# Last stage: GpSimd adds the first three of a token's six rows, VectorE the other three

## What is computed

```
for each expert e:  routed += combine[:, e] * (silu(g) * u @ down[e].T)      # six experts per token
sh = silu(xf @ shared_gate_w.T) * (xf @ shared_up_w.T)
shared_out = sh @ shared_down_w.T
x = x + gb * (routed + shared_out)                                           # gb: one row per batch
```

## Time and profile before

| | |
|---|---|
| time, median of 3 runs | 1427.1 us (1426.59 to 1427.19) |
| the profiled execution | 1430.49 us, its span in the trace 1428.7 us |
| busy over the span | PE 1359.2 us (95%), DVE 1129.7 (79%), ACT 754.5 (53%), POOL 606.7 (42%) |
| the last stage | from about 1333 us to the end |
| in it, loads of six rows | 16 of 1536 KB, median 8.6 us from issue to landing |

### The profile page before, as it was taken

One profiled execution on the slowest core, in us unless ns is written; L12 is line 12 of the kernel. 1 busy time (PEld: TensorE's weight loads), 2 busy tenths in 40 slices (PEclk: granted clock), 3 DMA queues, 4 the chain that ended last, 5 costly groups with the idle time before them and its releaser, 6 DMA issues.

```text
span 1428.7 us, 30863 instructions
## 1 busy us (share of the span) xinstructions
PE 1359.2 (95%) x8207; PEld 677.6 (47%) x8208; DVE 1129.7 (79%) x2815; ACT 754.5 (53%) x1155; POOL 606.7 (42%) x782
## 2 busy tenths in 40 slices
PE   7997999999999999999999999989999999999996
PEld 3552223332333323333333233558788888887552
DVE  7886999999999999999999992656566666665477
ACT  3772577667666767676667677113333333333100
POOL 4000113233744725546346366327755555555200
PEclk9997799999999999999999999999999999999998
DMA  6887355534346435454465346837766656555788
GB/s 213 273 266 201 102 165 134 112 91 106 99 127 166 103 101 140 124 135 101 112 162 146 80 134 198 257 124 237 226 202 203 203 168 189 180 173 173 270 304 317
DMA packets 216960, 243.55 MB, mean 170 GB/s; under 512 B 93949, under 2 KB 181501, under 8 KB 216738
## 3 DMA queue, kind: packets, MB, share of 16 engines
q1 hardware_dynamic: 189330, 166.42, 42.8%
q0 software_dynamic: 21776, 68.07, 13.4%
q10 hardware_dynamic: 5760, 7.87, 1.7%
HBM read 133.98 MB, written 108.28 MB: 170 GB/s over the span
## 4 chain that ended last, share of the span: by engine, by line
PE 68%; DVE 14%; DMA 5%; issue 2%; SPq 1%; ACT 1%; POOL 0%; DVEq 0%; POOLq 0%
PE psO L1171 14%; PE ex_psGU L1670 13%; PE psE L1158 13%; PE psM L1148 9%; DVE piece_max L1046 9%; PE ex_psY L1685 6%; PE ex_psX L1661 3%; PE psM L505 2%; PE co_psS L1935 2%; PE ex_psA L1679 2%; DMA wide<-results 1%; DMA results<-vals_inv,places 1%; PE psGU L1486 1%; PE late_psGU L1915 1%; PE psM L524 1%
## 5 line engine op out<-in xcount | busy, mean ns | idle before, releaser
L1046 DVE TENSOR_REDUCE piece_max<-psM 128x1 f32<-128x512 f32 x1024 | 642.2, 681 | 28.6 <-PE psM L1148 25.3
L1112 ACT ACTIVATE wide<-psE 128x1024 f32<-128x1024 f32 x512 | 497.1, 1021 | 208.4 <-PE psE L1158 206.2
L1148 PE MATMUL psM<-wide 48*128 48x512 bf16 x1024 | 324.5, 396 | 20.4 <-DVE piece_max L1046 12.0
L1158 PE MATMUL psE<-wide 49*128 49x512 bf16 (+1 forms) x2048 | 331.0, 382 | 2.4 <-DMA wide<-maxima 2.4
L1752 POOL DMA_INDIRECT results<-vals_inv,places x223 | 213.9, 959 | 155.9 <-DVE vals_inv L1738 89.9
L1171 PE MATMUL psO<-wide 128*32 128x512 f32 x2048 | 275.4, 610 | 0.6 <-ACT wide L1112 0.6
L1148 PEld LDWEIGHTS psM<-wide 48*128 48x128 bf16 x1024 | 78.2, 93 | 348.4 <-DVE piece_max L1046 275.8
L1670 PE MATMUL ex_psGU<-wide,ex_xT 128*128 x892 | 233.0, 384 | 0.6 <-ACT ex_xT L1703 0.6
L1158 PEld LDWEIGHTS psE<-wide 49*128 49x128 bf16 (+1 forms) x2048 | 117.9, 95 | 94.0 <-issue 10.4
L1670 PEld LDWEIGHTS ex_psGU<-wide,ex_xT 128*128 128x128 f32 x892 | 153.1, 192 | 15.6 <-issue 2.9
L1703 ACT ACTIVATE ex_xT<-ex_psX 128x256 f32<-128x256 f32 x223 | 85.6, 384 | 123.7 <-PE ex_psX L1661 122.5
(11 more groups left out here) (280 smaller groups left out, 1271.8 us busy)
## 6 DMA issues: line engine op xcount, KB each, us to landing
wide<-qk_parts SPq DMA_DIRECT2D x384, 64.0 KB
wide<-results SPq DMA_DIRECT2D x16, 1536.0 KB, 8.6
rows<-lists SPq DMA_DIRECT2D x112, 160.0 KB
h2Ts<-lists SPq DMA_DIRECT2D x111, 160.0 KB
qk_parts<-parts SPq DMA_DIRECT2D x32, 384.0 KB, 3.0
xin<-in_x_dram SPq DMA_DIRECT2D x16, 512.0 KB, 4.0
v_values<-vst SPq DMA_DIRECT2D x32, 256.0 KB, 3.6
wide<-v_values SPq DMA_DIRECT2D x16, 512.0 KB
```

The source lines that it names most:

```text
L1046: v.tensor_reduce(piece_max[:, qh, (x * PAIRS + h) * KT // QH + qt, kh:kh + 1], bank_of("piece", PIECES * group + n), AX.X, ALU.max, negat ...
L1112: nc.scalar.activation(probs[:, step % 2, 2 * pair:2 * pair + 2], psE[:, pair], ACT.Exp, scale=HD ** -0.5).then_inc(exp_ok, 1)
L1148: nc.tensor.matmul(bank_of(*user), qa[g][rows, h, qt * P:(qt + 1) * P], ka[g][rows, h, kh * 512:(kh + 1) * 512], start=True, stop=True).th ...
L1158: mm = nc.tensor.matmul(psE[:, pair, x], k[g][part, pair, kt * P:(kt + 1) * P], q[g][part, pair, qh * 512:(qh + 1) * 512], start=(q is qa) ...
```

## The change

PE's `add_half` and its PSUM tile go. GpSimd gets a block of its own in this stage: for each chunk two additions in SBUF, row 1 to row 0 and then row 2 to row 0, with a wait between them. DVE still adds rows 3 to 5, then waits for GpSimd's half, adds it from SBUF where it read `psS` in PSUM, and goes on as before. PE does only the late work, and that work is listed earlier on DVE (`beside`), while ACT's silu(2, 1) moves from behind the store of chunk 2 to behind that of chunk 3.

```
--- before.py
+++ after.py
@@ -1781,7 +1781,6 @@
     BUFS = 4
-    SUMS = 2
     SC = SHARED // P
...
@@ -1794,8 +1793,7 @@
         half = TOPK // 2
-        added, halves_done, halves_read, ch = (env.sem("co_" + n) for n in ("added", "halves_done", "halves_read", "chain"))
-        psS = ctx.enter_context(nc.psum_tensor("co_psS", [P, SUMS, WIDE, D], F32))
+        added, halves_done, ch, chain_p = (env.sem("co_" + n) for n in ("added", "halves_done", "chain", "chain_p"))
         six_in, stored = ([env.sem(f"co_{n}{u}") for u in range(BUFS)] for n in ("six_in", "stored"))
@@ -1837,16 +1835,27 @@
                     wait(act, y_done, k - 1)
                 nc.scalar.activation(act_s[k % 2][:, m], psGU[:, bank(k, m, 0)], ACT.Silu).then_inc(silu_ok, 1)
 
+            SILU_BEHIND = {0: (1, 1), 1: (2, 0), 3: (2, 1)}
             for k, m in ((0, 0), (0, 1), (1, 0)):
                 late_silu(k, m)
             for n, c in enumerate(order):
                 u = n % BUFS
                 act.wait_ge(added, n + 1)
                 act.dma_start(out[c], result[:, u]).then_inc(stored[u], 16)
-                if n in (0, 1, 2):
-                    late_silu(*((1, 1), (2, 0), (2, 1))[n])
+                if n in SILU_BEHIND:
+                    late_silu(*SILU_BEHIND[n])
             for u in range(BUFS):
                 act.wait_ge(stored[u], 16 * ((NCH - u + BUFS - 1) // BUFS))
+
+        @block.gpsimd
+        def _(pool):
+            chain = Chain(pool, chain_p)
+            g = nc.gpsimd
+            for n in range(NCH):
+                u = n % BUFS
+                pool.wait_ge(six_in[u], 16 * (n // BUFS + 1))
+                chain.link(g.tensor_tensor(six[:, u, :, 0], six[:, u, :, 0], six[:, u, :, 1], ALU.add))
+                g.tensor_tensor(six[:, u, :, 0], six[:, u, :, 0], six[:, u, :, 2], ALU.add).then_inc(halves_done, 1)
 
         @block.vector
         def _(dve):
@@ -1868,17 +1877,18 @@
                 v.tensor_tensor(x2, psL[:], x2, ALU.add).then_inc(y_read, 1)
 
             def beside(n):
-                if n == 1:
+                if n == 0:
+                    multiply_late(1, 0)
+                elif n == 1:
                     add_late(0)
-                    multiply_late(1, 0)
+                    multiply_late(1, 1)
                 elif n == 2:
-                    multiply_late(1, 1)
+                    add_late(1)
+                elif n == 3:
+                    multiply_late(2, 0)
                 elif n == 4:
-                    add_late(1)
-                    multiply_late(2, 0)
+                    multiply_late(2, 1)
                 elif n == 5:
-                    multiply_late(2, 1)
-                elif n == 7:
                     add_late(2)
 
             dve.wait_ge(env.closing_y_done, env.closing_chunks)
@@ -1895,8 +1905,7 @@
                 for j in range(half + 1, TOPK):
                     chain.link(v.tensor_tensor(six[:, u, :, half], six[:, u, :, half], six[:, u, :, j], ALU.add))
                 dve.wait_ge(halves_done, n + 1)
-                v.tensor_tensor(six[:, u, :, half], six[:, u, :, half], psS[:, n % SUMS], ALU.add).then_inc(halves_read, 1)
-                dve.wait_ge(halves_read, n + 1)
+                chain.link(v.tensor_tensor(six[:, u, :, half], six[:, u, :, half], six[:, u, :, 0], ALU.add))
                 chain.link(v.tensor_tensor(six[:, u, :, half], six[:, u, :, half],
                                            env.modb[:, b, 3].unsqueeze(1).to_broadcast([P, WIDE, D]), ALU.mult))
                 wait(dve, stored[u], 16 * (n // BUFS))
@@ -1927,14 +1936,6 @@
                                               start=(m == 0), stop=(m == SC - 1))
                 mm.then_inc(y_done, 1)
 
-            def add_half(n):
-                u = n % BUFS
-                pe.wait_ge(six_in[u], 16 * (n // BUFS + 1))
-                wait(pe, halves_read, n - SUMS + 1)
-                for j in range(half):
-                    mm = nc.tensor.matmul(psS[:, n % SUMS], env.ident[:], six[:, u, :, j], start=(j == 0), stop=(j == half - 1))
-                mm.then_inc(halves_done, 1)
-
             pe.wait_ge(env.x_ok, TILES)
             pe.wait_ge(env.act_ok, TILES)
             for m, side in ((0, 0), (0, 1), (1, 0), (1, 1)):
@@ -1942,24 +1943,16 @@
             late_in(1, 0, 0)
             pe.wait_ge(env.a_ok, TILES)
             pe.wait_ge(env.y_ok, TILES)
-            add_half(0)
             late_out(0)
-            add_half(1)
             late_in(1, 0, 1)
             late_in(1, 1, 0)
-            add_half(2)
             late_in(1, 1, 1)
             late_in(2, 0, 0)
-            add_half(3)
             late_out(1)
             late_in(2, 0, 1)
-            add_half(4)
             late_in(2, 1, 0)
             late_in(2, 1, 1)
-            add_half(5)
             late_out(2)
-            for n in range(6, NCH):
-                add_half(n)
 
 
 def declare(nc, env, ctx):
```

More of the change, by code:

```diff
@@ L1928, in late_out @@
                 mm.then_inc(y_done, 1)
[L1930 to L1936, removed]
             pe.wait_ge(env.x_ok, TILES)
```

## The result

The changed kernel takes 1439.88 us (median of 4 runs, 1436.92 to 1441.88) against 1427.14 us (4 runs, 1426.59 to 1431.11): a ratio of 1.008, with a 95% interval of 1.0062 to 1.0097. The forecast was 1439.6 us. The profiled execution of the change took 1436.92 us with a span of 1435.2.

A forecast was written before the change was run, and what follows sets the result against it. PE held the last stage's first half, then loads led. Chunk 0's start 1347.9 + DVE's work 63.1 + turns 27.5 + last store 2.7 gave span 1441.2, 12.5 above 1428.7; added to the median, 1439.6 us, range 1431 to 1449.

The forecast's parts named there:

- Start: Start of the last stage: PE's and DVE's late work goes first, so DVE begins chunk 0 at 1347.9, not 1344.40.
- Turns: Last stage: DVE's two-SBUF-input additions and GpSimd's additions exclude each other; 25 GpSimd operations cost 27.5 us.
- two handovers: Each engine's next operation after the other's end: GpSimd's takes 1.13 us, DVE's 0.54, read from two places in the trace.
- Price: Cost to DVE per GpSimd operation in the last stage: between 0.95 and 1.36 us, taken as 1.1.
- DVE's own work: Last stage from 1347.9: 56.0 us for 16 chunks, 5.9 of late work, 1.2 of waiting for silu; 63.1 us.
- new wait for silu(2, 1): Before chunk 4 DVE stands for ACT's silu, now behind chunk 3's store: an estimated 1.2 us.
- PE's clock: Last stage: PE is done by about 1380 and its clock no longer matters; late_out(0) was put at 3.62 us.
- Loads: Last stage: DVE and GpSimd need 5.7 us per chunk, more than a load's 4.77, so loads no longer decide.
- Sum: Whole kernel: span 1441.2 us, 12.5 more than 1428.7; with that added to the runs' median, 1439.6 us.
- A: Rival for the last stage: DVE and GpSimd work side by side, the change is faster, 1418.5 us; chance 0.10.
- B: Rival for the last stage: partial blocking at 0.5 to 0.75 us per GpSimd operation, 1424.6 to 1430.9 us; chance 0.08.
- C: Rival for the last stage: GpSimd works only when DVE stops for it, 1445.8 us; chance 0.22 together with full prices.

The follow-up runs named there:

- e1: The changed kernel with DVE's running sum of a chunk kept in PSUM, so only its first operation has two SBUF inputs; ratio 0.9971 to the kernel before.
- e3: The changed kernel with GpSimd's two additions per chunk replaced by memsets that read nothing, rows 0 to 2 left out; ratio 0.9944 to the kernel before.
- e8: The changed kernel with each GpSimd addition cut into two of 128x256, one per token of the pair; ratio 1.0048 to the kernel before.
- e7: The changed kernel with running sums in PSUM, row 3 copied there by ACT, silu(2, 1) behind chunk 2's store again; 1417.76 us, ratio 0.9932 to before.
- e2: The kernel before with only the change's new order of late work on DVE and ACT, PE still adding; ratio 1.0056 to the kernel before.

## Why the prediction was right

**Start.** Chunk 0 was to begin on DVE 9.7 us after the first load's issue (1347.9 - 1338.2). It began at 1343.58, 9.65 after 1333.93. Right.

**Turns.** Read from two short operations of the trace, and right in kind: whole instructions, in both directions, for reads (e1, e3, e8). The two handovers taken from there, 1.13 us for GpSimd after DVE and 0.54 for DVE after GpSimd, came out at 1.12 and 0.54.

**Price.** I had a low end of 0.95 us, with each side's start-up hidden behind the other, and a high end of 1.36, and took 1.1. A single operation of DVE that was blocked lost 0.94 (1.63 - 0.69): the low end was the right account, and neither 1.1 nor the whole 1.276 us of GpSimd's operation was paid. This is the mis-sized term: 27.5 us for turns, measured 24.8. At that price it is 24.8 / 0.94 = 26 turns where I had 25; the count is derived, not read off one by one. For the same reason chunks did not come 5.6 to 5.8 us apart, as the prediction's list of signs says: from chunk 6 on they came 5.2 apart in the mean ((1428.85 - 1381.99) / 9), and 5.39 where a chunk met two turns.

**DVE's own work.** Last operation's end at 1431.74 + 0.69 = 1432.43 in the timeline, less 1343.58, less the turns: 64.0 us, where I had 63.1. The new wait for silu(2, 1) was 1.2 as estimated. The missing 0.9 is DVE's wait of 1.2 for the third late_out, less 0.3 elsewhere. Here a step of the prediction was wrong: PE's clock was said to matter no longer, but that late_out took 5.66 us at a granted clock of 0.65 and not 3.62.

**Loads.** They were to stop deciding, and they did: in the stage's second half DVE is busy 54.33 of 55.90 us, and GpSimd, not DVE, waits for loads (45.1 us). The prediction gave a landing 6.2 to 8.6 us and passed over the longest of the earlier trace rows, 17.7; in the change the longest was 17.3, and DVE waited for none.

**Sum.** A stretch of 103.0 us was forecast (1441.2 - 1338.2) and 101.3 and 101.5 were measured: 2.7 too much for turns, 1 too little for waits. Carried over to the median this should have left the forecast 1.6 us high. It is 0.3 low, since two things differ from run to run. The first load was issued at 1338.21 and 1334.26 in two traces of the kernel before and at 1333.93 and 1337.59 in two of the change. And the stage before took 90.5 and 88.1 us in those two, so that it grew by 10.8 to 13.4, where 12.5 was forecast from the first alone. So the closeness of 1439.6 to 1439.88 is partly luck; what is shown is the stage, to about 2 us.

**Rivals.** A, no turns, is excluded for this change, but its sum came out where the turns were removed: 81.9 us in e3 and 81.1 in e7. B is excluded by the price, 0.94 us where it needed 0.75 or less, and C by the absence of any wait of L1908 for GpSimd. What the forecast did not see is the cost of the new order to PE's version (e2). That had no part in the result.

## What to carry to other kernels

Before handing an elementwise job to GpSimd beside a busy VectorE, count VectorE's instructions that read two SBUF tensors: each that meets a reading GpSimd instruction waits for much of it (0.94 of 1.26 us here), and no semaphore wait in the profile says so; only the lengths do. Putting one operand in PSUM, here the running sum itself, takes the collision away at about 0.01 us an operation (0.70 against 0.69). That alone turned a loss of 0.8% into a gain of 0.3% (e1), and with the first operand copied there by ScalarE and silu(2, 1) moved back it was 0.7% (e7). And a hand-written order of one engine has to be tried against the queue of the engine that feeds it.

## What the runs showed of the hardware that I had not expected

- A turn costs the blocked DVE operation GpSimd's whole length less 0.32 us, at both lengths: 1.26 - 0.94 in the change, and 0.72 - 0.40 in e8, where 0.72 is the shortest that L1858 ran.
- A memset of 128x1536 on GpSimd, 1.377 us, costs VectorE's two-input operations beside it nothing (688 and 692 ns).
- With PE idle the granted clock stood at 0.55 over 55.9 us, near the lower of its two levels (1.2 of 2.4 GHz). The matmuls of late_out issued after a pause took 5.36 and 5.66 us, the latter at a granted clock of 0.65, where the kernel before, whose PE did not pause ahead of them, took 3.62 for each: moving work off PE made what was left there slower.
